# A retention layer with blockwise FP4 feed-forward: clamp in a seventeenth column, and masking two heads on VectorE and six by way of ScalarE and GpSimd

## The reference

```
q, k = rope(x @ Wq), rope(x @ Wk)            # 8 heads of 16
v, g = x @ Wv, x @ Wg                        # 8 heads of 32
scores = (q / 4) k^T * decay_h^(i-j), i >= j # no softmax
o = scores @ v;  o = o * rsqrt(mean(o*o) + eps) * g_norm_w
x1 = layernorm(x + (o * silu(g)) @ Wo)

quant(a): per block of 16: scale = max(max|a| / 6, 1e-12)
          nearest of 0, .5, 1, 1.5, 2, 3, 4, 6 to |a / scale|, * sign * scale
h  = silu(quant(x1) @ quant(Wgate)^T) * (quant(x1) @ quant(Wup)^T)    # 352 wide
out = layernorm(x1 + quant(h) @ quant(Wdown)^T)
```

## Time and profile before

| | |
|---|---|
| median of 3 runs | 153.95 us (153.28 to 154.63) |
| profiled execution: its time, its span | 154.49 us, 152.8 us |
| VectorE busy | 130.1 us, 85% |
| TensorE matmuls busy (weight loads) | 125.0 us, 82% (76.6 us) |
| GpSimd busy | 101.2 us, 66% |
| ScalarE busy | 95.3 us, 62% |
| chain that ended last | VectorE 55%, TensorE 26% |

### The profile page before, as it was taken

How to read it: one execution, slowest core, us unless ns; L and a number is a source line. 1 busy time by engine, 2 the same in 40 slices (tenths; PEclk the granted TensorE clock), 3 DMA queues, 4 the chain that set the end, 5 groups by cost and what they waited for, 6 DMA issues and landing times.

```text
span 152.8 us, 3517 instructions
## 1 busy us (share of the span) xinstructions
PE 125.0 (82%) x1206; PEld 76.6 (50%) x1206; DVE 130.1 (85%) x466; ACT 95.3 (62%) x279; POOL 101.2 (66%) x139
## 2 busy tenths in 40 slices
PE   0309887999999989999999999999999967768630
PEld 0104343746656455656565656565656545445420
DVE  0075997995899999999999999999999899999840
ACT  1204745768676867767676767676767764754581
POOL 4010389595856869695858597979797966734660
PEclk9999999999999999999999999999999999999995
DMA  3899930000000000000000000000000000000123
GB/s 120 269 379 394 394 100 0 0 2 6 0 0 4 0 0 6 2 0 4 0 0 4 0 0 2 4 2 0 4 0 0 4 0 2 17 17 17 34 75 116
DMA packets 6404, 7.57 MB, mean 50 GB/s; under 512 B 667, under 2 KB 5531, under 8 KB 6259
## 3 DMA queue, kind: packets, MB, share of 16 engines
q1 hardware_dynamic: 5712, 6.42, 12.2%
q10 hardware_dynamic: 675, 0.94, 2.0%
HBM read 6.31 MB, written 1.05 MB: 48 GB/s over the span
## 4 chain that ended last, share of the span: by engine, by line
DVE 55%; PE 26%; issue 5%; DMA 5%; POOL 3%; ACT 3%; ACTq 1%; POOLq 0%; DVEq 0%
DMA wgu_nat<-in_w_gate_up 5%; DVE h_grid L638 4%; DVE h L768 4%; PE ps L312 4%; DVE hs L617 4%; PE ps L329 4%; DVE probs L698 4%; DVE h_plus L634 3%; DVE xs L621 3%; DVE h_ratio L629 3%; DVE rope_s L692 3%; DVE stats L723 3%; PE ps L305 2%; DVE rope_c L690 2%; DVE ms L715 2%
## 5 line engine op out<-in xcount | busy, mean ns | idle before, releaser
L864 POOL TENSOR_TENSOR rstd_h<-ms,minus_half 128x8 f32<-128x8 f32 x16 | 26.5, 1654 | 19.3 <-DVE ms L715 19.3
L875 POOL TENSOR_TENSOR rstd<-veps,minus_half 128x1 f32<-128x1 f32 x32 | 18.5, 588 | 3.4 <-DVE veps L731 3.3
L312 PE MATMUL ps<-w_vg,xT 128*128 128x512 f32 x32 | 18.5, 662 | 2.5 <-DVE r L736 2.5
L855 POOL TENSOR_TENSOR qk<-rope_c,rope_s 128x256 f32<-128x256 f32 x16 | 14.4, 902 | 9.0 <-DVE rope_s L692 9.0
L482 ACT ACTIVATE q_eo<-ps,consts 128x128 f32<-128x128 f32 x32 | 11.8, 370 | 8.4 <-PE ps L321 8.4
L452 PE MATMUL ps<-wd_T,hT 128*128 128x128 f32 x96 | 13.7, 279 | 2.7 <-ACT hT L481 2.7
L305 PE MATMUL ps<-w_qk,xT 128*128 128x256 f32 x32 | 11.8, 451 | 4.6 <-DMA w_qk<-in_w_qk 4.6
L452 PEld LDWEIGHTS ps<-wd_T,hT 128*128 128x128 f32 x96 | 12.1, 192 | 6.0 <-DVE r L746 2.6
L541 ACT ACTIVATE o_sq<-ps 128x256 f32<-128x256 f32 x16 | 6.2, 385 | 14.2 <-PE ps L377 14.1
L888 POOL TENSOR_TENSOR hq<-h_grid,hs 128x352 f32<-128x352 f32 x16 | 13.0, 811 | 3.1 <-DVE h_grid L638 3.1
L436 PE MATMUL ps<-wgu_T,xqT 128*128 128x352 f32 x32 | 13.6, 508 | 1.0 <-DVE r L746 1.0
(11 more groups left out here) (98 smaller groups left out, 348.8 us busy)
## 6 DMA issues: line engine op xcount, KB each, us to landing
tabs<-rope_tables SPq DMA_DIRECT2D x1, 1536.0 KB, 12.9
out<-x SPq DMA_DIRECT2D x16, 64.0 KB, 1.6
tabs<-rope_tables SPq DMA_DIRECT2D x1, 960.0 KB, 9.3
xT<-x_transposed SPq DMA_DIRECT2D x1, 512.0 KB, 10.2
x_res<-x SPq DMA_DIRECT2D x1, 512.0 KB, 14.0
tabs<-rope_tables SPq DMA_DIRECT2D x1, 384.0 KB, 8.4
wgu_nat<-in_w_gate_up ACTq DMA_DIRECT2D x1, 352.0 KB
xT<-x_transposed SPq DMA_DIRECT2D x1, 320.0 KB, 7.7
```

Of the source, the lines that this page charges most:

```text
L312: mm(vg_ps, xT[:, c * C:(c + 1) * C], w_vg[:], start=True, stop=True).then_inc(vg_pe, 1)
L855: gp.tensor_tensor(qk[:, c % D, :], rope_c[:, c % D, :], rope_s[:, c % D, :], ALU.add).then_inc(qk_p, 1)
L864: gp.tensor_tensor(rstd_h[:, c, :], ms[:, c, :], minus_half[:], ALU.pow).then_inc(rms_p, 1)
L875: gp.tensor_tensor(rstd[n][:, c, :], veps[n][:, c, :], minus_half[:, 0:1], ALU.pow).then_inc(ln_p[n], 1)
```

## The change

It has three parts.

The clamp of the scale: x1 and h are stored with a seventeenth element behind each block of sixteen, which holds `LEAST` = 6e-12. The maximum over seventeen elements is then never below it, and the instruction that divided by 6 and clamped (`quant_scale`) is left out for x and h; its factor goes into the ratio and into the weights' values.

The mask: `MB` = 1. VectorE masks bank 0, two heads; ScalarE copies banks 1 to 3, and GpSimd selects six heads.

The orders of all four engines' lists are new, as are the stages at which the weights' steps stand.

```diff
+MB = 1
+LEAST = 6e-12
-        x1 = sb("x1", 128, NC, H)
+        x1_blocks = sb("x1_blocks", 128, NC, XB, BLK + 1)
+        x1 = lambda c: x1_blocks[:, c, :, 0:BLK]
-        h = sb("h", 128, 2, I)
+        h_blocks = sb("h_blocks", 128, 2, HB, BLK + 1)
+        h = lambda c: h_blocks[:, c % 2, :, 0:BLK]
-        FIRST, LAST = -5, 32
+        FIRST, LAST = -3, 35
...
-                if tile.get(bank) == "sc" and bank < 2:
+                if tile.get(bank) == "sc" and bank < MB:
                     pe.wait_ge(mask_v, filled["sc"])
...
                 free_scores_bank(0)
+                free_scores_bank(1)
                 tile[0] = tile[1] = "oT"
...
-                    if n == NH // 2:
+                    if n == 2 * MB:
                         pe.wait_ge(mask_p, c + 1)
```

The new lists, TensorE, ScalarE, VectorE and GpSimd in this order (the old ones stand in the listing above):

```diff
+                run(transpose_o, 0)
+                run(transpose_qk, 1)
+                run(up, -4)
                 if s == 3:
                     transpose_down_weights()
                 if s == 2:
                     transpose_gate_up_weights()
                 run(project_vg, 1)
                 run(transpose_xq, -3)
                 run(scores, 1)
                 run(project_qk, 2)
+                run(down, -7)
+                run(gate, -3)
+                run(transpose_y, 0)
+                run(from_state, 1)
+                run(state_product, 1)
+                run(values, 1)
+                run(transpose_h, -6)
+                run(out_projection, 0)
...
+                run(copy_scores, 2)
+                if s == -2:
+                    weights_magic(0)
+                run(ln1_centre, 0)
+                if s == 1:
                     copy_gate_up_weights()
+                run(magic_x, -1)
+                run(silu_of_gate, -2)
+                run(ln2_norm, -19)
+                run(copy_yT, 1)
+                run(copy_oT, 2)
+                run(ln1_norm, 0)
+                run(squares, 2)
+                run(q_odd, 3)
+                run(q_even, 3)
+                run(copy_hT, -5)
+                if s == 0:
+                    weights_magic(1)
+                run(k_transposed, 3)
                 if s == 1:
                     copy_down_weights()
+                run(magic_h, -3)
+                run(copy_v_and_silu, 3)
+                run(copy_xqT, -1)
...
+                run(gated, 1)
+                run(h_product, -3)
                 if s == -2:
+                    weights_amax(1)
+                run(x_inv, -1)
+                if s == 0:
+                    weights_value(0)
+                if s == 1:
+                    weights_plus(1)
+                run(ln2_aggr, -7)
+                run(ln1_aggr, 0)
+                run(x_ratio_, -1)
+                run(h_plus_, -4)
                 if s == 1:
                     weights_grid(1)
                 if s == -1:
+                    scale_wo()
                 if s == -1:
                     weights_grid(0)
                 run(mask_scores, 2)
+                run(ln1_eps, 0)
                 run(rotate, 3)
+                run(h_amax, -3)
+                if s == -2:
+                    weights_plus(0)
+                run(ln2_sum, -6)
+                run(h_inv, -3)
                 run(next_state, 2)
                 run(x_plus_, -1)
+                if s == 1:
+                    weights_value(1)
+                run(h_grid_, -4)
                 if s == -1:
+                    weights_inv(1)
+                run(x_grid_, -1)
+                run(h_ratio_, -3)
+                run(ln2_eps, -7)
+                run(ln2_stats, -6)
+                if s == -1:
+                    weights_ratio(1)
+                run(ln1_sum, 1)
+                run(x_amax, 0)
+                run(mean_square, 2)
+                if s == -3:
+                    weights_amax(0)
+                if s == -3:
+                    weights_inv(0)
+                run(ln1_stats, 1)
+                if s == -3:
+                    weights_ratio(0)
...
+                run(h_value, -5)
+                run(rms_rstd, 1)
+                run(gated_output, 1)
+                run(mask_scores, 2)
+                run(rotate_add, 3)
+                run(ln1_rstd, 0)
                 run(ln2_rstd, -10)
+                run(x_value, -1)
```

More of the change, by code:

```diff
@@ L28 @@
 NUDGE = 1.0 - 2.0 ** -22
+LEAST = 6e-12
 LN = ["sum", "stats", "aggr", "eps"]
-QUANT = ["amax", "scale", "inv", "ratio", "plus", "grid"]
+QUANT = ["amax", "inv", "ratio", "plus", "grid"]
 def constants():
@@ L126, in seq_postln_kernel @@
         probs = sb("probs", 128, 2, NH, C)
-        raw = sb("raw", 128, 2, NP, C)
+        raw = sb("raw", 128, 2, NH - 2 * MB, C)
         S = sb("S", 128, 2, 2 * DV)
@@ L530, in copy_scores @@
                 act.wait_ge(sc_pe, c + 1)
-                copy(raw[:, c % 2, :, :].rearrange("p (j e) q -> p j (e q)", j=2), ps[:, 2:4, 0:256]).then_inc(
+                copy(raw[:, c % 2, :, :].rearrange("p (j e) q -> p j (e q)", e=2), ps[:, MB:4, 0:256]).then_inc(
                     raw_act, 1)
@@ L583, in _ @@
                 run = stage_runner(s)
[L584 to L591, removed]
-                    copy_gate_up_weights()
[L593 to L597, removed]
-                run(ln2_norm, -16)
-                if s == 1:
-                    weights_magic(1)
-                run(silu_of_gate, -3)
-                run(ln1_centre, -1)
-                run(copy_yT, 0)
-                run(ln1_norm, -1)
-                run(copy_oT, 1)
-                if s == 2:
+                run(copy_scores, 2)
[3 more added lines that the diff above has]
+                if s == 1:
+                    copy_gate_up_weights()
+                run(magic_x, -1)
[11 more added lines that the diff above has]
+                run(k_transposed, 3)
+                if s == 1:
                     copy_down_weights()
+                run(magic_h, -3)
+                run(copy_v_and_silu, 3)
+                run(copy_xqT, -1)
         @block.vector
@@ L642, in wq_views @@
                 src, rows, cols, dst = ((wgu_nat, WR, 2 * WT * H, wgu_q), (wd_nat, 128, I, wd_q))[n]
-                small = [wr_small[0:rows, n, m, 0:cols // BLK] for m in range(3)]
+                small = [wr_small[0:rows, n, m, 0:cols // BLK] for m in range(4)]
                 return (src[:, 0:cols], small, *(a[n][0:rows, 0:cols] for a in (wr_ratio, wr_magic, wr_plus)),
@@ L670, in weights_value @@
                 _, small, ratio, _, _, dst = wq_views(n)
+                dve.wait_ge(wquant_v[n]["inv"], 2)
                 dve.wait_ge(wquant_v[n]["grid"], 1)
-                vec.tensor_tensor(blocks(dst), blocks(ratio), spread(small[1], blocks(ratio)), ALU.mult).then_inc(
+                vec.tensor_tensor(blocks(dst), blocks(ratio), spread(small[3], blocks(ratio)), ALU.mult).then_inc(
                     wq_v[n], 1)
@@ L745, in ln2_sum @@
                 dve.wait_ge(down_pe, c + 1)
-                vec.tensor_tensor(r[1][:, c, :], down_ps, x1[:, c, :], ALU.add).then_inc(ln_v[1]["sum"], 1)
+                vec.tensor_tensor(blocks(r[1][:, c, :]), blocks(down_ps), x1(c), ALU.add).then_inc(ln_v[1]["sum"], 1)
             def ln2_stats(c): ln_stats(1, c)
@@ L858, in mask_scores @@
                 pool.wait_ge(raw_act, c + 1)
-                gp.affine_select(out=probs[:, c % 2, 4:, :], in_=raw[:, c % 2, :, :], compare_op=ALU.is_ge, fill=0.0,
-                                 base=0, pattern=[[0, NP], [1, C]], channel_multiplier=-1).then_inc(mask_p, 1)
+                gp.affine_select(out=probs[:, c % 2, 2 * MB:, :], in_=raw[:, c % 2, :, :], compare_op=ALU.is_ge, fill=0.0,
+                                 base=0, pattern=[[0, NH - 2 * MB], [1, C]], channel_multiplier=-1).then_inc(mask_p, 1)
             def rms_rstd(c):
```

113 lines of the change are left out of this document (28 added, 85 removed).

## The result

The changed kernel takes 147.3 us (median of 4 runs, 146.5 to 147.52) where the kernel before takes 154.29 (4 runs, 153.28 to 154.71): ratio 0.9553, 95% interval 0.9497 to 0.9609. It is faster, by 1.1 us more than forecast and inside the range. The profiled execution took 146.5 us with a span of 144.8. It is the fastest of the four, and the one before lay a little above its median, so the two profiles differ by 8.0 us where the medians differ by 7.0.

The account below looks back on a forecast made before the run. VectorE was taken to set the period, TensorE close behind. Gains of 2.8 + 2.5 + 0.3 + 1.8 less 1.9 made 5.5 us off 154.49, 149.0, adjusted to the runs' median: 148.4 us; range 145.0 to 152.5.

Parts of the forecast that it names:

- Who sets the pace: Middle stages: VectorE sets the 7.59 us period before; TensorE sets the next, VectorE's surplus becoming a wait before `next_state`.
- The middle: Chunk 8's to chunk 15's score matmuls: period falls to 7.19 us, 0.40 us in each of 7 stages, 2.8 us gained.
- The stretches: VectorE instructions beside GpSimd's two-input ones run long: `h_ratio` 1.05 us, scale of x 0.49; removing scales saves 0.48 per stage.
- The mask: Per stage: VectorE masks 256 columns instead of 512, 0.25 us less; ScalarE's copy 0.22 more, GpSimd's select at most 0.32 more.
- The fill: Chunk 1 to chunk 8, seven steps: new ScalarE and TensorE orders gain 0.35 us each, 2.5 us.
- The start: First chunks: gate and up weights' maximum now stands behind `rotate(0)`; 0.3 us gained, bounds -0.3 and 1.0.
- The drain: Chunk 15's scores to its hT copy: removed scales and `transpose_h` one stage closer gain 1.8 us, bounds 0.3 and 2.8.
- The tail: After the last hT: fourteen outputs remain instead of ten, issued by SyncE 0.47 us apart; 1.9 us lost.
- A: Rival: GpSimd's stretches find other victims, VectorE keeps the pace, period 7.5 us; 153.5 us, chance 0.15.
- B: Rival: values of heads 2 to 7 come late, TensorE waits 0.6 us per stage; 156.9 us, chance 0.07.
- C: Rival: fill, start and drain reach 4.2, 1.0 and 2.8, the middle 2.9; 145.0 us, chance 0.10.
- the signs of being right: Period 7.1 to 7.3 us, VectorE under 95% waiting before `next_state`, no projection wait for `ln1_sum`, hT(15) at 137 to 139 us.

Follow-up runs that it names:

- the split experiment: Changed kernel with `transpose_y` moved between `from_state` and `state_product` on TensorE; median 148.58 us, ratio 0.966 to the kernel before, period 6.98 us.
- the place of `up`: Changed kernel with `up` moved back from behind the q/k transposes to behind `values`; median 153.94 us, ratio 0.995 to the kernel before, period 7.42 us.
- four and four: Changed kernel with the mask split in equal halves again (`MB` = 2); median 148.52 us, ratio 0.951 to the kernel before, period 6.91 us.
- q in two parts: Changed kernel with `q_even` moved behind `k_transposed` and `magic_h` on ScalarE; median 149.37 us, ratio 0.962 to the kernel before, period 7.04 us.
- the order of `down` and `gate`: Changed kernel with `gate` ahead of `down` on TensorE from stage 15 on; median 147.72 us, ratio 0.960 to the kernel before, drain 28.4 us.

## Why the prediction was right, and where it was off

The direction and the main mechanism were right. The closeness of the total is partly luck, since a middle forecast too low and a drain forecast too high cancel.

**Who sets the pace: right in the main.** VectorE's list before, TensorE's after, with VectorE's wait before `next_state` as named. Removing either the scale or its stretch took the period from 7.59 to 7.19 us. Two things were missed. Before, it is not the amount of VectorE's work that counts, for the mask alone took 0.3 us of it away and left 7.6; by the rows of the clamp-only kernel the pace is that of a round through VectorE and GpSimd, a reading that no run tested. And after, TensorE is not quite alone: in each stage a weight load waits 0.38 us for `ln1_sum`, which was to be a sign of being wrong, though the matmuls ahead of it cover nearly all of it.

**The middle, 2.8 us forecast and 5.4 found: mis-sized.** The failed step is "its own floor is thus about 7.07 + 0.11 = 7.18 us", taken over to the new list. The old list's floor was nearly right (7.07 in the mask-only kernel), but a floor belongs to a list, not to an engine. Of the 0.36 us between 7.18 and 6.82, 0.11 are the error in the old floor, whose stretch from 93.74 to 100.81 still held a weight load that came late, and 0.25 are the shorter list. I priced the order's waits and did not price what the order does to TensorE itself: the split experiment puts one more turn to a part of the array and back at 0.15 us a stage, and the place of `up` is worth 0.59. The bound of 0.5 us a stage was too low too; 0.77 were gained.

**The stretches: the right mechanism, more than I took.** I let `h_ratio` keep its stretch in the sum. In the new orders it is gone, and already with the new orders alone `h_ratio` takes no more than 0.52 us in any chunk. What I had not seen is that a stretch keeps itself up, as it depends on which of the two engines begins first, and that in the old orders it passes from one instruction to another, `h_grid`, `h_ratio` or `x_grid`.

**The mask: right sizes, little effect.** 0.25 us a stage were counted as part of VectorE's relief. The sum did not rest on them, since TensorE bounded it. The experiment with four and four confirms that but for 0.1 us a stage.

**The fill, 2.5 forecast and 3.6 found.** The orders carry it: 42.7 us with the orders alone, 45.6 with the other two parts in the old ones. The cause named first, ScalarE's order of q, is not it (42.2 with q in two parts); the place of `up` is 1.8 us of it. Another 0.7 us are no gain at all: the old list does `down(0)` ahead of chunk 8's scores, where my fill ends, and the new one behind them. What gives the remaining 1.1 us was not tried.

**The start, 0.3 forecast and 1.3 found.** The profiles' means differ by 0.3, which their scatter does not tell from nothing.

**The drain, 1.8 us forecast and 0.4 lost: wrong.** The step was that the scales give back 0.08 us and 0.1 to 0.4, and that `transpose_h` "now runs one stage closer". In the old orders the clamp gains 0.6 us there (27.4 to 26.8). The new orders lose that and more: the changed kernel has 27.8, and the clamp is worth 1.6 us there, by the two kernels with the mask four and four. Some 0.7 us of the drain are `down(7)`, which the new list puts behind the scores from which I measured; they come out of the fill, and like for like the drain gained a quarter of a microsecond. `transpose_h` one stage closer does not show as a gain: the last but one stage is 0.7 us longer than in the old orders. What holds that stage up is the order of `down` and `gate`, as the experiment shows; why the stages before it do not shorten is open.

**The tail, 1.9 us lost: right**, counted from fourteen outputs in place of ten at SyncE's pace, and shown by taking it away.

**The rivals.** A's mechanism exists, but the new orders turn it round: `h_ratio` begins at 85.41, ahead of `x_value` at 85.57, and keeps its 0.52 us, and it is `x_value` that takes 0.61 us where its shortest in the mask-only kernel is 0.40. B did not come: values of the later heads waited for the select 0.4 us in the whole execution. C's 145.0 us were not reached, and its terms were others: its middle of 2.9 us was far exceeded, and its drain of 2.8 did not come. Of the signs of being right, the period (7.1 to 7.3 us) and the time of the last hT (137 to 139) were missed on the fast side, by 6.82 and 135.87; the rest came but for the load's wait told above.

## What to carry to other kernels

An engine's time per stage is a property of its instruction order, not only of its instructions: before bounding a reordered kernel by the next-fullest engine, count what the new order changes on that engine, above all changes between whole and partial arrays on TensorE, and which matmul covers another engine's copy. When an instruction takes two or three times what its form takes elsewhere, look at what GpSimd does beside it and which of the two began first; moving the one instruction was here worth as much as removing it. A relief on the fullest engine can bring nothing, as the mask alone did up to chunk 11: ask whether the relieved instruction stands in the round that sets the pace. And count what is left in the in-order queues behind the last critical step: offsets that cost nothing in the middle decide the tail.

## What the runs showed of the hardware

- One program can have two steady states in one execution: 7.6 and then 7.07 us a stage in the mask-only kernel, according to whether GpSimd's two-input instructions begin ahead of VectorE's (`x_grid` 0.81 or 0.28 us, the scale 0.48 or 0.16).
- The granted clock falls from its upper level, 2.4 GHz, to the lower, 1.2 GHz (0.50 of it) near the end, and not always at the same point. In the changed kernel it falls between 139 and 140 us, behind the last matmul, which ends at 137.4. In the one with the mask four and four it falls between 136 and 137 us, while matmuls are still running, although its TensorE was busier from 130 to 140. The two rows below are these ten microseconds in the changed kernel and in that one.

```profile
130.00:140.00 10.00, 4.89 (x33) 3.88 (x33) 6.37 (x26) 6.27 (x20) 5.79 (x9) 0.99 0.16 48
```

```profile
130.00:140.00 10.00, 7.06 (x37) 5.53 (x38) 6.25 (x24) 4.75 (x14) 6.19 (x9) 0.81 0.05 14
```
